# Self-attention on Trainium2: the last chunk of a pair's maxima taken one step earlier, and negated there

## The chip, the cores and the metric

The kernel runs on one core of a Trainium2 chip. The metric is the device time of one execution in microseconds, given as the median of several runs.

## The reference

A decoder layer in float32 for four sequences of 1024 tokens of width 256, in three parts, each followed by a residual sum and a layer norm: causal self-attention with 16 heads of 64 and rotary embedding, cross-attention that gathers at computed places, and a feed-forward part with fake quantisation. The change touches only the first:

```
q = (x @ wq.T + bq).reshape(Bx, Sx, H, DK).transpose(0, 2, 1, 3)     # k, v alike
q, k = _rope(q, k)
scores = jnp.einsum('bhqd,bhkd->bhqk', q, k)
scores = jnp.where(causal[None, None], -jnp.inf, scores)
attn = jax.nn.softmax(scores / math.sqrt(DK), axis=-1)
out = jnp.einsum('bhqk,bhkd->bhqd', attn, v)                         # then @ wo.T + bo
```

## The kernel before

Self-attention takes the first 1510 us or so of the program. Its work is cut into 16 groups (`GROUPS`: four sequences times four groups of four heads), and a group into two pairs of heads (`PAIRS` = 32 in all; pair `n` belongs to group `i = n // 2`, with `p = n % 2`). Both heads of a pair are worked on together.

The softmax is computed on transposed scores (keys on the partitions), so the maximum of each query has to be known before. It is found by a first, separate product of queries and keys: the nine `CHUNKS`, each a PSUM slot of 128 x 1024 values that holds one or two tiles of queries for both heads. TensorE writes a chunk (`max_chunk`, matmuls at L394), VectorE adds the causal mask where the chunk has corners (L633) and reduces it (L639, or L644 for parts of unequal width) in `maximum`. After the last chunk `negate` joins the halves (L650) and writes the negated maxima (`negmax`, L653).

In the pair itself, TensorE turns the negated maxima into a row in PSUM (`max_row`, L406), ScalarE copies the row (L507), and the row is added to every unit of scores by a second matmul (`shift`, L424) on top of the product of keys and queries (`scores`, L416). There are twelve such units (`NU`), two per step; s0 to s11 below. ScalarE takes the exponential of each (L518), GpSimd masks those on the diagonal (L761) and adds all up for the softmax's sums (L780), and TensorE weighs the values (`weigh`, L440).

A pair has six steps (`STEPS`, `m` = 0 to 5). The order of a step on TensorE is written out by hand: scores of units 2m and 2m+1; at step 0 the row of maxima and the last two weighings of the pair before; the two shifts; the weighings of the two units before; the chunks of the next pair's maxima that `CHUNKS_AT[m]` names; and one unit of other work (`FULL_AT`: projection of the next group's queries and keys at steps 0 to 3 of the first pair, output projection of the last group and values of the next at steps 0 to 3 of the second, L337 to L378). Steps 4 and 5 have no such unit.

All these outputs except those of `weigh` go through one ring of three PSUM slots of two banks (`SLOTS`), in the order that `slot_order` lists. `wait_slot` makes each use wait until the use three places before it has been read: scores by ScalarE's exponential, a chunk by VectorE's reduction (`s_mread`), the row by ScalarE's copy, a projection of queries and keys by VectorE's rotation. TensorE executes in program order, so whatever stands behind a waiting use waits with it.

VectorE's order is written by hand too: in each step the chunks of `CHUNKS_AT[m]`; at step 5 `negate`; then splits of the weights (`split`, L592 and L595: a float32 value as the sum of two parts), statistics or row normalisation of finished rows, the rotation or the values, at steps 4 and 5 of some pairs two pieces each of the split of x, and at step 4 `normalise` (L666), which multiplies the outputs of pair n-1 by the inverses of the sums. The split of x stands in pairs 5, 13 and 21, for the next sequence, and its last piece is needed by the projection of queries and keys in the next pair.

SyncE's queue stacks the rotated queries and keys into the operands (`stack`, L251). Before that it waits until all the scores of the pair that still uses them are done (`s_s`). After the split of x it loads the x of the sequence after (L243), which stands ahead of a stacking in the queue.

Of the kernel before, what the change touches and what calls it, by code (L numbers as in the profile page):

```python
# [27 lines left out]
PAIRS = 2 * GROUPS  # L28
# [4 lines left out]
NCH = len(CHUNKS)  # L33
PARTS = 2
STEPS = NU // 2
CHUNKS_AT = [range(0, 0), range(0, 2), range(2, 4), range(4, 6), range(6, 8), range(8, 9)]
QK_UNITS = 4
V_UNITS = 2
OUT_UNITS = 2
# [30 lines left out]
def slot_order():  # L70
# [3 lines left out]
    for n in range(PAIRS):  # L74
        i, p = divmod(n, 2)
        for m in range(STEPS):
# [3 lines left out]
            if n + 1 < PAIRS:  # L80
                order += [("max", n + 1, c) for c in CHUNKS_AT[m]]
            if FULL_AT[p][m]:
# [11 lines left out]
def attention(nc, dram, y, psum):  # L94

    ctx = ExitStack()
    with ctx:
# [217 lines left out]
        def _(pe):  # L315
# [67 lines left out]
            def max_chunk(n, c):  # L383

                p = n % 2
                if n == 0 and c == 0:
                    pe.wait_ge(s_top, 16 * STACK_DMAS)
                if c == (2 if n == 0 else 0):
                    pe.wait_ge(s_ops[p], 16 * STACK_DMAS * (n // 2 + 1))
                wait_slot(pe, "max", n, c)  # L390
                dst = slot("max", n, c)
                for qt, hf, col, width in chunk_parts(c):
                    for hh, rows in enumerate(HEADS):
                        last = nc.tensor.matmul(dst[:, hh, col:col + width], ops[p][rows, 0, qt * P:(qt + 1) * P],  # L394
                                                ops[p][rows, 1, hf * BANK:hf * BANK + width], start=True, stop=True)
                last.then_inc(s_m, 1)
# [67 lines left out]
            for n in range(PAIRS):  # L464
                i, p = divmod(n, 2)
                for m in range(STEPS):
# [13 lines left out]
                    if n + 1 < PAIRS:  # L480
                        for c in CHUNKS_AT[m]:
                            max_chunk(n + 1, c)
# [75 lines left out]
        def _(dve):  # L558
# [38 lines left out]
            def split_x(b, piece):  # L597
                hf, kt = divmod(piece, KT)
                if b and piece == 0:
                    dve.wait_ge(s_x, 16 * b)  # L600
                tok = HALVES[hf]
                split(xT[:, kt, tok], xT_hi[:, kt, tok], xT_lo[:, kt, tok], s_xs)

            def split_qk(i):
                dve.wait_ge(s_wqk, 32 * (i + 1))
                split(wqk[:, :, :], wqk_hi[:, :, :], wqk_lo[:, :, :], s_wqks)

            def split_v(i):
                dve.wait_ge(s_wv, 32 * (i + 1))
                split(wv[:, :, :], wv_hi[:, :, :], wv_lo[:, :, :], s_wvs)  # L610
# [11 lines left out]
            def maximum(n, c):  # L622

                dve.wait_ge(s_m, NCH * n + c + 1)
                src = slot("max", n, c)
                parts = chunk_parts(c)
                corners = causal_corners(c)
                if corners:
                    blocks = src.rearrange("p h (k q) -> p h k q", q=P)
                    step = corners[1] - corners[0] if len(corners) == 2 else 1  # L630
                    block = blocks[:, :, corners[0]:corners[-1] + 1:step, :]
                    mask = later[:, :].unsqueeze(1).unsqueeze(1).broadcast_to([P, 2, len(corners), P])
                    V.tensor_tensor(block, block, mask, ALU.add).then_inc(s_mmask, 1)  # L633
                    dve.wait_ge(s_mmask, len(MASKED) * n + MASKED.index(c) + 1)
                if parts[0][3] == parts[-1][3]:
                    place_of = [qt + TT // 2 * hf for qt, hf, col, width in parts]
                    step = place_of[-1] - place_of[0] if len(parts) == 2 else 1
                    width = parts[0][3]
                    V.reduce_max(maxes[:, :, place_of[0]:place_of[-1] + 1:step],  # L639
                                 src[:, :, 0:len(parts) * width].rearrange("p h (k q) -> p h k q", q=width),  # L640
                                 AX.X).then_inc(s_mread, PARTS)
                else:
                    for qt, hf, col, width in parts:
                        V.reduce_max(maxes[:, :, qt + TT // 2 * hf], src[:, :, col:col + width], AX.X)\  # L644
                         .then_inc(s_mread, PARTS // len(parts))

            def negate(n):

                dve.wait_ge(s_mread, PARTS * NCH * (n + 1))
                V.tensor_tensor(maxa[:, :, TT // 2:TT], maxa[:, :, TT // 2:TT], maxb[:, :, :], ALU.max).then_inc(s_mcomb, 1)  # L650
                dve.wait_ge(s_mcomb, n + 1)
                dve.wait_ge(s_row, n)
                V.tensor_scalar(negz[:, :, :, 0], maxa[:, :, :], -1.0, None, ALU.mult).then_inc(s_neg, 1)  # L653

            def invert(n):
                dve.wait_ge(s_dcol, 32 * (n + 1))
                dve.wait_ge(s_rrow, 16 * n)
                V.reciprocal(rcol[:, :, :], dcol[:, :, :]).then_inc(s_rcol, 1)
# [9 lines left out]
            def residual(i, u):  # L668

                b = i // NG  # L670
                dst = y[:, b * TT + u * (TT // 2):b * TT + (u + 1) * (TT // 2), :]
                if i % NG == 0:
                    dve.wait_ge(s_y, 16)
                    V.tensor_tensor(dst, dst, out_bias[:, :].unsqueeze(1).broadcast_to([P, TT // 2, E]), ALU.add)\
                     .then_inc(s_yb, 1)
                    dve.wait_ge(s_yb, OUT_UNITS * b + u + 1)
                dve.wait_ge(s_out, OUT_UNITS * i + u + 1)
                if i:
                    dve.wait_ge(s_res, OUT_UNITS * (i - 1) + u + 1)
                V.tensor_tensor(dst, dst, slot("out", i, u).rearrange("p h (t e) -> p (h t) e", e=E), ALU.add)\  # L680
                 .then_inc(s_res, 1)

            def row_statistics(b, half):

                dve.wait_ge(s_res, OUT_UNITS * NG * (b + 1))
                for t in range(4 * half, 4 * half + 4):
                    V.bn_stats(a_stats[:, t, :], y[:, b * TT + t, :]).then_inc(s_as, 1)
                if half:
                    dve.wait_ge(s_as, TT * (b + 1))
                    for t in range(TT):  # L690
                        ins = V.bn_aggr(a_mv[:, t, :], a_stats[:, t, :])
                    ins.then_inc(s_avar, 1)

            def normalise_rows(b, half):
                dve.wait_ge(s_astd, b + 1)
                for t in range(4 * half, 4 * half + 4):
                    ins = V.tensor_scalar(y[:, b * TT + t, :], y[:, b * TT + t, :], a_mv[:, t, 0:1], a_rstd[:, t:t + 1],
                                          ALU.subtract, ALU.mult)
                ins.then_inc(s_ax1, 1)
# [13 lines left out]
            for n in range(PAIRS):  # L713
                i, p = divmod(n, 2)
                for m in range(STEPS):
                    if n + 1 < PAIRS:
                        for c in CHUNKS_AT[m]:
                            maximum(n + 1, c)
                    if m == STEPS - 1 and n + 1 < PAIRS:
                        negate(n + 1)  # L720
                    if n == 0 and m == 0:
                        split_qk(1)
                    if p == 1 and m == 0:
                        if i + 1 < GROUPS:
                            split_v(i + 1)
                        if i >= NG and i % NG >= 2:
                            normalise_rows(i // NG - 1, i % NG - 2)
                    if p == 1 and m < 2 and i >= NG and i % NG == 1:
                        row_statistics(i // NG - 1, m)
                    if p == 1 and m == 1 and i + 2 < GROUPS:  # L730
                        split_qk(i + 2)
                    if FULL_AT[p][m]:
                        kind, u = FULL_AT[p][m]
                        if kind == "out" and i:
                            residual(i - 1, u)
                        if kind == "qk" and i + 1 < GROUPS:
                            rotate(i + 1, u)
                        if kind == "v" and i + 1 < GROUPS:
                            values(i + 1, u)
                    if p == 1 and m >= 4 and i % NG == 2 and i // NG + 1 < B:  # L740
                        for piece in range(2):
                            split_x(i // NG + 1, 2 * (m - 4) + piece)
                    if m == 2 and n:
                        invert(n - 1)
                    if m == 4 and n:
                        normalise(n - 1)
# [1548 lines left out]
```

## Time and profile before

| | |
|---|---|
| median of 3 runs | 2374.44 us (2371.68 to 2383.48) |
| the profiled execution | 2374.92 us |
| its span, first to last instruction | 2373.2 us |
| mean granted TensorE clock | 0.917 |
| TensorE busy | 1896.3 us (80%) |
| VectorE busy | 1580.8 us (67%) |
| GpSimd busy | 1175.9 us (50%) |
| ScalarE busy | 913.5 us (38%) |

An engine's busy time is a sum over the whole span; what an edit is worth has to be read from the stage in which it stands. In the timelines below a line gives the start in us, the duration in us (of a merged run of equal instructions, first start to last end), the engine, the line, the operation, and in brackets how long the engine was idle before it and which instruction released it. A TensorE clock of 1.00 is 2.4 GHz and of 0.50 is 1.2 GHz.

### The profile page before, as it was taken

The numbers are of one execution on the slowest core, as the hardware profiler recorded it, in microseconds if no ns is written. First come the engines' busy times: TensorE is split into PE (matmuls) and PEld (weight loads), VectorE is DVE, ScalarE is ACT, GpSimd is POOL, SyncE is SP. The second block draws the span as 40 slices with busy tenths as digits, with TensorE's granted clock in tenths as the row PEclk, the third lists the DMA queues.
The fourth block names the chain that finished last, engine by engine and source line by source line (L and its number), as shares of the span: only waits on it lengthen the run. The fifth ranks groups of instructions, "written<-read, shape, count | busy, mean of one in ns | idle before, by whom it ended". The sixth has DMA issues, their size and how long they took to land. (4 is left out here: it accounts for less than half of the span.)

```text
span 2373.2 us, 41594 instructions
## 1 busy us (share of the span) xinstructions
PE 1896.3 (80%) x16891; PEld 1130.9 (48%) x16891; DVE 1580.8 (67%) x2581; ACT 913.5 (38%) x1273; POOL 1175.9 (50%) x938
## 2 busy tenths in 40 slices
PE   6888878888878888888888898658787778884476
PEld 3444434444445444444444443446565566663332
DVE  6765656656656657666666663267868768778676
ACT  0222222222222222222222223156675765775376
POOL 0455436545644554555465456136555454646247
PEclk7999989999989999999999999779898898888686
DMA  7122112112221121121131121200000000100002
GB/s 216 28 57 52 41 52 70 41 39 56 54 56 41 43 65 41 43 65 37 39 72 39 39 47 34 59 5 7 2 2 7 2 2 2 41 2 2 2 1 71
DMA packets 57407, 93.39 MB, mean 39 GB/s; under 512 B 26624, under 2 KB 39040, under 8 KB 52864
## 3 DMA queue, kind: packets, MB, share of 16 engines
q1 hardware_dynamic: 48000, 90.47, 15.1%
q8 instruction: 134, 2.20, 0.4%
q10 hardware_dynamic: 9216, 0.27, 0.2%
q14 instruction: 57, 0.47, 0.1%
HBM read 52.43 MB, written 4.46 MB: 24 GB/s over the span
## 5 line engine op out<-in xcount | busy, mean ns | idle before, releaser
L780 POOL TENSOR_TENSOR acc<-acc,probs 128x1024 f32<-128x1024 f32 (+3 forms) x320 | 553.7, 1730 | 143.7 <-ACT probs L518 114.9
L518 ACT ACTIVATE probs<-psum 128x1024 f32<-128x1024 f32 (+3 forms) x384 | 290.5, 808 | 639.0 <-PE psum L424 639.0
L416 PE MATMUL psum<-operands 64*128 64x512 f32 (+3 forms) x1536 | 316.1, 517 | 59.8 <-DVE turned L587 23.5
L639 DVE TENSOR_REDUCE maxes<-psum 128x2 f32<-128x1024 f32 (+1 forms) x224 | 268.3, 1223 | 132.0 <-PE psum L394 121.8
L1322 ACT ACTIVATE onehot<-psum 128x1024 bf16<-128x1024 f32 x320 | 322.8, 1037 | 1.3 <-PE psum L1132 1.3
L1150 PE MATMUL psum<-pieces,onehot 128*128 128x64 bf16 x7680 | 296.1, 201 | 30.9 <-ACT vs L1329 24.1
L1150 PEld LDWEIGHTS psum<-pieces,onehot 128*128 128x128 bf16 x7680 | 267.6, 103 | 96.7 <-issue 46.5
L440 PE MATMUL psum<-probs,vals 128*64 128x512 f32 (+3 forms) x1536 | 293.8, 505 | 4.4 <-POOL probs L761 4.4
L1736 POOL TENSOR_TENSOR vs<-vs,wgt 128x1280 f32<-128x1280 f32 x64 | 156.9, 2452 | 261.4 <-DVE wgt L1579 261.4
L761 POOL TENSOR_SCALAR_AFFINE_SELECT probs<-probs 128x256 f32<-128x256 f32 x256 | 132.1, 528 | 278.2 <-ACT probs L518 278.2
L416 PEld LDWEIGHTS psum<-operands 64*128 64x128 f32 x1536 | 131.9, 187 | 202.2 <-issue 86.3
L777 POOL COPY acc<-probs 128x1024 f32<-128x1024 f32 x64 | 66.5, 1038 | 318.1 <-ACT probs L518 318.1
L1539 DVE TENSOR_TENSOR prod<-psum,xq 128x320 f32<-128x320 f32 x256 | 123.6, 488 | 114.3 <-PE psum L1150 109.5
L1132 PE MATMUL psum<-i0T,near 32*128 32x512 bf16 x640 | 133.5, 420 | 80.1 <-ACT onehot L1322 74.1
L633 DVE TENSOR_TENSOR psum<-psum,later 128x512 f32<-128x512 f32 (+1 forms) x160 | 93.8, 586 | 148.9 <-PE psum L394 148.9
L579 DVE SCALAR_TENSOR_TENSOR turned<-psum,bqk,rot 128x512 f32<-128x512 f32 x128 | 90.1, 745 | 146.4 <-PE psum L341 101.6
L1329 ACT ACTIVATE vs<-psum 128x320 f32<-128x320 f32 x256 | 114.8, 448 | 156.5 <-DVE prod L1539 156.2
L440 PEld LDWEIGHTS psum<-probs,vals 128*64 128x64 f32 x1536 | 95.6, 140 | 141.2 <-issue 131.6
L394 PE MATMUL psum<-operands 64*128 64x512 f32 (+3 forms) x768 | 118.0, 397 | 54.6 <-DVE turned L587 44.5
L378 PE MATMUL psum<-wo,ctxT 128*128 128x256 f32 x512 | 119.9, 388 | 26.9 <-ACT probs L518 15.7
L394 PEld LDWEIGHTS psum<-operands 64*128 64x128 f32 x768 | 59.9, 190 | 155.4 <-issue 89.5
L532 ACT ACTIVATE den_rows<-psum 128x1024 f32<-128x1024 f32 x32 | 32.8, 1024 | 250.5 <-PE psum L452 250.5
(220 smaller groups left out, 3181.4 us busy)
## 6 DMA issues: line engine op xcount, KB each, us to landing
operands<-turned SPq DMA_DIRECT2D x124, 256.0 KB, 4.3
rden<-inverse_rows SPq DMA_DIRECT2D x64, 256.0 KB, 3.8
wqk<-in_wqk SPq DMA_DIRECT2D x16, 512.0 KB, 3.2
wv<-in_wv SPq DMA_DIRECT2D x16, 256.0 KB, 2.6
y<-in_x SPq DMA_DIRECT2D x1, 4096.0 KB, 20.5
wo<-in_wo SPq DMA_DIRECT2D x16, 256.0 KB, 2.6
out<-res SPq DMA_DIRECT2D x16, 256.0 KB, 2.1
xT<-in_xT SPq DMA_DIRECT2D x3, 1024.0 KB, 6.7
```

What stands on the lines that cost most here:

```text
L394: last = nc.tensor.matmul(dst[:, hh, col:col + width], ops[p][rows, 0, qt * P:(qt + 1) * P], ops[p][rows, 1, hf * BANK:hf * BANK + width], ...
L416: nc.tensor.matmul(dst[:, hh, 0:width], ops[n % 2][rows, 1, kt * P:(kt + 1) * P].bitcast(F32), ops[n % 2][rows, 0, a:a + width].bitcast(F3 ...
L440: last = nc.tensor.matmul(obank[rows, hf, a - hf * BANK:BANK], vals[i % 2][:, kt, 2 * p + hh, :], probs[u % PBUF][:, hh, 0:width], start=k ...
L518: nc.scalar.activation(probs[u % PBUF][:, :, 0:width], slot("s", n, u)[:, :, 0:width], ACT.Exp, scale=1.0 / D ** 0.5).then_inc(s_exp, 1)
L639: V.reduce_max(maxes[:, :, place_of[0]:place_of[-1] + 1:step], src[:, :, 0:len(parts) * width].rearrange("p h (k q) -> p h k q", q=width), ...
L761: G.affine_select(block, block, [[0, 2], [1, P]], ALU.is_ge, 0.0, base=0, channel_multiplier=-1)\
L780: G.tensor_tensor(dst, dst, src, ALU.add).then_inc(s_acc, 1)
L1132: last = nc.tensor.matmul(bc[m % 2][:, hf * BANK:(hf + 1) * BANK], near[row:row + Q, NK * j + k, :], i0T[row:row + Q, hp // 2, :], start=T ...
L1150: last = nc.tensor.matmul(out, onehot[:, n % 2, k, tok:tok + P], pieces[b % 2][p][:, h, :, :].rearrange("p (s c) d -> p s (c d)", s=2), st ...
L1322: A.activation(onehot[:, n % 2, k, :], bc[m % 2], ACT.Relu).then_inc(s_oh, 1)
L1539: V.tensor_tensor(prod[u % 2][:, :, :].rearrange("p t (k d) -> p t k d", d=HD), slot("s", n, u)[:, :, 0:W].rearrange("p t (k d) -> p t k d ...
L1736: G.tensor_tensor(v, v, w.broadcast_to([P, TT * NK * 2, HD]), ALU.mult).then_inc(s_wm, 1)
```

## The change

The ninth chunk (number 8) of the next pair's maxima moves from step 5 to step 4, in the ring's order, on TensorE and on VectorE, since all three loops read `CHUNKS_AT`. The negation moves on VectorE from step 5 to step 4, right behind that chunk. TensorE's row stays where it is, in step 0 of the next pair.

```
-CHUNKS_AT = [range(0, 0), range(0, 2), range(2, 4), range(4, 6), range(6, 8), range(8, 9)]
+CHUNKS_AT = [range(0, 0), range(0, 2), range(2, 4), range(4, 6), range(6, 9), range(9, 9)]
...
                     if n + 1 < PAIRS:
                         for c in CHUNKS_AT[m]:
                             maximum(n + 1, c)
-                    if m == STEPS - 1 and n + 1 < PAIRS:
+                    if m == STEPS - 2 and n + 1 < PAIRS:
                         negate(n + 1)
```

The uses of the ring around the end of a pair, before and after:

```
before: s8 s9 max6 max7 | s10 s11 max8 | s0 s1 row ...
after:  s8 s9 max6 max7 max8 | s10 s11 | s0 s1 row ...
```

## Rows read from the trace of the kernel before

**Rows 1.** The page, busy time of each engine (share of the span) xinstructions.

```profile
PE 1896.3 (80%) x16891; PEld 1130.9 (48%) x16891; DVE 1580.8 (67%) x2581; ACT 913.5 (38%) x1273; POOL 1175.9 (50%) x938
```

**Rows 2.** Waits, 0 to 1560 us: who waited for whom, us in total, times, longest.

```profile
PE psum L406 <- DVE negmax L653: 58.0, 32, 5.6
```

**Rows 3.** Timeline of PE, 774 to 812 us, row of pair 16.

```profile
790.70 0.64 PE L406 MATMUL psum<-ident,negmax 128*64 128x128 bf16 x16 [1.68 <-DVE negmax L653]
```

**Rows 4.** Timeline of DVE, 774 to 812 us, ahead of pair 16.

```profile
785.36 1.29 DVE L644 TENSOR_REDUCE maxes<-psum 128x2 f32<-128x256 f32 x2
786.57 1.96 DVE L666 TENSOR_TENSOR ctxT<-osum,rden 128x1024 f32<-128x1024 f32 x1
```

**Rows 5.** Timeline of all engines, 733 to 755 us, into pair 15.

```profile
740.71 1.23 DVE L639 TENSOR_REDUCE maxes<-psum 128x2 f32<-128x1024 f32 x1 [0.67 <-PE psum L394]
...
741.99 0.49 PE L416 MATMUL psum<-operands 64*128 64x128 f32 x4 [0.67 <-DVE maxes L639]
...
742.57 1.29 DVE L644 TENSOR_REDUCE maxes<-psum 128x2 f32<-128x256 f32 x2
...
743.78 1.57 DVE L666 TENSOR_TENSOR ctxT<-osum,rden 128x1024 f32<-128x1024 f32 x1
...
744.23 0.50 PE L394 MATMUL psum<-operands 64*128 64x512 f32 x2
...
744.57 1.67 PE L416 MATMUL psum<-operands 64*128 64x512 f32 x8
...
745.27 0.42 DVE L633 TENSOR_TENSOR psum<-psum,later 128x256 f32<-128x256 f32 x1
...
747.26 0.20 DVE L653 TENSOR_SCALAR negmax<-maxes 128x16 bf16<-128x16 f32 x1
...
747.52 0.64 PE L406 MATMUL psum<-ident,negmax 128*64 128x128 bf16 x16 [1.29 <-DVE negmax L653]
```

**Rows 6.** Timelines of DVE and of PE, 88 to 101 us, into pair 1.

```profile
92.68 1.29 DVE L644 TENSOR_REDUCE maxes<-psum 128x2 f32<-128x256 f32 x2
...
97.50 0.64 PE L406 MATMUL psum<-ident,negmax 128*64 128x128 bf16 x16 [1.16 <-DVE negmax L653]
```

**Rows 7.** Timelines of DVE, SyncE and PE, 676 to 722 us, into pair 14.

```profile
693.87 0.69 DVE L595 TENSOR_TENSOR xT_low<-xT,xT_high 128x512 fp32r<-128x512 f32 x1
...
706.21 1.41 DVE L579 SCALAR_TENSOR_TENSOR turned<-psum,bqk,rot 128x512 f32<-128x512 f32 x2 [11.64 <-DMA operands<-turned]
...
695.27 4.60 SPq L251 DMA_DIRECT2D operands<-turned  x4
...
710.53 1.33 PE L394 MATMUL psum<-operands 64*128 64x128 f32 x6 [6.73 <-DVE turned L587]
```

**Rows 8.** Timelines of DVE and of PE, 1053 to 1085 us, into pair 22.

```profile
1056.07 1.29 DVE L644 TENSOR_REDUCE maxes<-psum 128x2 f32<-128x256 f32 x2
...
1066.63 0.69 DVE L595 TENSOR_TENSOR xT_low<-xT,xT_high 128x512 fp32r<-128x512 f32 x1
...
1065.29 1.06 PE L406 MATMUL psum<-ident,negmax 128*64 128x128 bf16 x16 [5.56 <-DVE negmax L653]
...
1069.38 0.47 PE L337 MATMUL psum<-xT_high,wqk_high 128*128 128x512 f32 x1 [0.89 <-ACT probs L518]
```

**Rows 9.** Two lines: duration ns min/median/max, first and last start.

```profile
L666 DVE TENSOR_TENSOR ctxT<-osum,rden x32: 1226/1612/2042, 130.1 to 1507.8; 128x1024 f32<-128x1024 f32 x32
...
L595 DVE TENSOR_TENSOR xT_low<-xT,xT_high x16: 691/692/1631, 31.5 to 1066.6; 128x512 fp32r<-128x512 f32 x16
```

**Rows 10.** Timeline of DVE, 774 to 812 us, the rotation in pair 16.

```profile
797.10 1.41 DVE L579 SCALAR_TENSOR_TENSOR turned<-psum,bqk,rot 128x512 f32<-128x512 f32 x2 [6.46 <-PE psum L341]
```

**Rows 11.** The page, DMA issues: count, KB each, median us to landing.

```profile
operands<-turned SPq DMA_DIRECT2D x124, 256.0 KB, 4.3
```

**Rows 12.** Two periods from row to row: busy us by engine, granted clock, DMA.

```profile
790.70:837.07 46.37, 39.11 (x218) 20.38 (x218) 32.19 (x45) 12.10 (x16) 23.20 (x21) 0.96 0.19 44
880.26:925.46 45.20, 37.52 (x217) 19.23 (x217) 32.09 (x45) 12.10 (x16) 23.18 (x21) 1.00 0.19 45
```

More of the change, by code:

```diff
@@ L35 @@
 STEPS = NU // 2
-CHUNKS_AT = [range(0, 0), range(0, 2), range(2, 4), range(4, 6), range(6, 8), range(8, 9)]
+CHUNKS_AT = [range(0, 0), range(0, 2), range(2, 4), range(4, 6), range(6, 9), range(9, 9)]
 QK_UNITS = 4
@@ L718, in _ @@
                             maximum(n + 1, c)
-                    if m == STEPS - 1 and n + 1 < PAIRS:
+                    if m == STEPS - 2 and n + 1 < PAIRS:
                         negate(n + 1)
```

## The prediction

> **What bounds the kernel now.** I read the page's busy times first: TensorE (PE) is busy 80% of the span, VectorE (DVE) 67% [rows 1]. A change that adds and removes no instruction can only move PE's waits. The list of waits, cut to the attention stage (0 to 1560 us), names the one near the change: the matmuls of the row of maxima (L406) stood 58.0 us in 32 places behind `negmax` (L653), 5.6 us at most [rows 2]. The timeline gives the single waits before these 32 groups: one of 0.47 (pair 0, outside the loop), one of 1.16 (pair 1), fifteen of 1.29 to 1.33 (pairs 3, 5, ..., 29 and pair 8), twelve of 1.67 to 1.75 (the other even pairs and pair 31) and three of 5.56 us (pairs 6, 14, 22); they sum to 58. Rows 3 and 4 show one of the twelve, rows 5 one of the fifteen, rows 8 one of the three.
>
> Why PE waits there: VectorE reduces chunk 6, masks and reduces chunk 7 (L633, L644), normalises the context (L666), masks and reduces chunk 8 and negates, without a gap of over 0.1 us, and PE starts 0.05 us after the last [rows 3 to 5]. The row is set by VectorE's queue.
>
> **The change part by part.** Nothing is added or removed. Two things move: on VectorE chunk 8 (0.42 + 1.23 us) and the negation go ahead of `normalise(n-1)` and, in three pairs, of splits of x; on PE the matmuls of chunk 8 go ahead of the scores of units 10 and 11 (s10, s11). The second also moves the uses of the PSUM ring of three slots, where a use waits for the reader of the use three places before. Before: s10 waits for the exponential of s9, s11 for the reduction of chunk 6, chunk 8 for chunk 7. After: chunk 8 waits for s9, s10 for chunk 6, s11 for chunk 7. That is a new wait: s11 is one place further on in VectorE's queue, and behind it in PE's order stand both shifts, the weighing of units 8 and 9, the next pair's s0 and s1, and then the row.
>
> A. The negation. VectorE can go on straight after chunk 7. From the mask of chunk 8 to the end of the negation it takes 745.27 to 747.46 = 2.19 us, so `negmax` is ready at 743.78 + 2.19 = 745.97 instead of 747.46 [rows 5].
>
> B. s11. Before, chunk 6's reduction ends at 740.71 + 1.23 = 741.94 and s11 starts at 741.99: 0.05 us from a reduction to PE. After, s11 starts at 742.57 + 1.29 + 0.05 = 743.91. From the start of s11 to the end of s1 PE needed 741.99 to 744.57 + 1.67 = 746.24, 4.25 us; of this chunk 8's matmuls (744.23 to 744.57, 0.34) now stand earlier: 3.91 us. The row then starts at 743.91 + 3.91 = 747.82, against 747.52: **+0.30 us** [rows 5]. The negation is 1.85 us ahead of it and no longer matters. Chunk 8's 0.34 us lie in the wait for chunk 6 (0.67 us before s11 [rows 5]) and cost nothing; uncovered they cost 0.34. s0 needs chunk 8 read, at 743.78 + 0.53 + 1.23 = 745.5, and starts at 747.82 - 1.67 = 746.15: covered by 0.6 us.
>
> C. The same for the twelve: 785.36 + 1.29 + 0.05 + 3.91 = 790.61 against 790.70: **-0.09 us** [rows 3, 4]. The two kinds differ in what the normalisation had cost, 1.57 or 1.96 us. Pair 1 has none: 92.68 + 1.29 + 0.05 + 3.91 = 97.93 against 97.50, +0.43 us [rows 6].
>
> Sum of the regular boundaries: 14 x 0.30 + 0.25 (pair 8, normalisation 1.61) + 0.43 - 12 x 0.09 = **+3.8 us**. What follows a row (ACT's copy, shifts, exponentials, projection) hangs on it, and the next rotation on VectorE waits for PE (6.46 us idle [rows 10]), so a delay of the row goes through in full. Ends: a reduction may reach PE 0.15 us earlier or later, 28 x 0.15 = 4 us to either side.
>
> D. Pairs 6 and 14. Here two splits stood ahead of the normalisation too. The row starts some 4 us earlier (by the like pair 22: 1056.07 + 1.29 + 0.05 + 3.91 = 1061.32 against 1065.29 [rows 8]). But nothing that ends last hangs on it: the next group's projection needs the last split, at the end of the same gapless VectorE queue (693.87 + 0.69 = 694.56 in either order); SyncE then issues xT and, from 695.27, the operands (4.60 us), the rotation waits for these until 706.21, and PE's maxima for the rotation until 710.53, idle for 6.73 us [rows 7]. The 4 us become a longer wait there. Worth 0, apart from E.
>
> E. Contention on VectorE in the same three places. The normalisation takes 1.23 to 2.04 us over the stage, 1.74 there; a split's subtraction 0.69 in the median and 1.63 at most [rows 9], the latter there, while GpSimd masks and adds. With 2.1 us of PSUM work moved to the front, the normalisation should stand behind the end of GpSimd's adds: 1.74 - 1.23 = 0.5 us for each of three. Ends: 0, and 0.5 + 2 x (1.63 - 0.69) = 2.4 us if the subtractions came free too; I take 0.5, since the adds move back as well, with the exponentials of units 10 and 11.
>
> The Trainium skill ("SBUF — State Buffer", section "Who interferes with whom") says that a VectorE instruction with two SBUF inputs contends with a GpSimd instruction that reads SBUF, while a reduction never does. By that rule no term of B or C could grow from GpSimd's moved adds, as both rest on reductions and on PE, and E may be anything between its ends. The trace agrees: 1.23 to 2.04 us for one form of normalisation [rows 9], 1.23 and 1.29 us for the reductions wherever they stand [rows 4 to 6].
>
> F. Pair 22 has the splits but no load of xT behind them. The next group's projection began at 1069.38 and needs the last split, done at 1066.63 + 0.69 = 1067.32 [rows 8]. The earlier row lets it start at 1067.4: -2.0, with E -2.5 us. Ends: 0 (if a low clock eats it) and -4.5.
>
> G. The SyncE queue. It holds the stacking of operands until all scores of a pair are done; s11 comes 743.91 - 741.99 = 1.9 us later, so do these four DMAs. Issued from 785.46 for 3.12 us, they land 4.3 us after each issue [rows 11], by 792.9, and 794.8 after; the rotation that needs them starts at 797.10, held by PE [rows 10]. Two us of cover: 0. Without it up to 1.9 us for each of 15 groups.
>
> **Sum**: +3.8 - 1.0 (E, pairs 6 and 14) - 2.5 = +0.3 us on the profiled execution's 2374.92 us (span 2373.2 and 1.7 around it). The median of the three runs is 2374.44, 0.5 lower; I predict **2375 us**, no change that a measurement of this kernel can tell (0.5%, 12 us).
>
> **Rivals.**
> 1. The wait is simply removed: 58.0 - 0.5 us go, 2317 us, if s10 and s11 don't bind. For it: the largest wait of PE for VectorE in this stage [rows 2]. Against: VectorE has no gap between chunk 6 and chunk 7, so s11 cannot start before 743.9. 6%.
> 2. Slower by TensorE's clock. PE's idle time now lies in one wait of 1.5 to 1.9 us at s11 soon after that of s10. The granted clock fell to 0.50 (1.2 GHz) in stretches after waits of this stage; a period with one such stretch (mean clock 0.96) took 46.37 us, one without (1.00) 45.20: 1.17 us each [rows 12]. If each of the 28 boundaries brought one more, 33 us: 2408. It decides from 10 boundaries on. For: the waits before s11 now come close together. Against: the idle time per boundary is the same sum, and 1.29 and 1.68 us in one piece mostly left the clock at 1.00. 7%.
> 3. The delayed stacking (G) comes to bind: 15 x 1.9 = 28 us at most, 2403. It decides only if landing takes 2.3 us more than now. 2%.
> 4. The change doesn't bring what it says, since PE asks for the negated maxima no earlier. That is my forecast in the regular pairs. A partial form, faster by the whole 4 us of pairs 6, 14 and 22, gives 2374.9 + 3.8 - 12 = 2367, still within 0.5%.
>
> **How the numbers follow.** Forecast (within 0.5%, with rival 4): 82%; rival 1: 6%; rival 2: 7%; rival 3: 2%; a gain I don't see: 3%. Faster 0.09, same 0.82, slower 0.09. Range: regular boundaries 4 us either way, the three split boundaries -8 to +3, low-clock stretches, which may come or go, some 6 us; and the runs of before themselves lie from 2371.68 to 2383.48. So 2366 to 2384.
>
> **What would show it.** The idle time before L406 behind `negmax` falls from 58 to under 2 us; that before L416 behind a maximum (L639, L644) grows to some 55 us; the row starts 3.9 us after s11; at pairs 6 and 14 PE's maxima still wait for a rotation that waited for the operands. I am wrong if s11 starts less than 1.5 us after s10, if the granted clock of the stage differs by over 0.02, or if the rotation begins to wait for DMA in ordinary groups.

## The result: slower, by TensorE's clock

The changed kernel takes 2414.96 us (median of 4 runs, 2411.64 to 2420.36) against 2378.96 us for the kernel before beside it: a ratio of 1.0179, 95% interval 1.0149 to 1.0208 (the two medians alone give 1.0151). I had predicted 2375 us in a range of 2366 to 2384, and given 7% to the rival that turned out to be the case. The profiled execution took 2411.64 us. Of the runs below, one of the kernel before (2946.74 us) and one of filled_wait (9743.97 us) stand far from all others and enter no ratio.

The page of the changed kernel, first its busy times, then the costliest groups (busy us, mean ns | idle before, us). The instruction counts are those of [rows 1]:

```profile
PE 1942.5 (81%) x16891; PEld 1141.2 (47%) x16891; DVE 1581.1 (66%) x2581; ACT 913.4 (38%) x1273; POOL 1175.9 (49%) x938
...
L416 PE MATMUL psum<-operands 64*128 64x512 f32 (+3 forms) x1536 | 333.0, 540 | 102.0 <-DVE maxes L644 38.0
...
L440 PE MATMUL psum<-probs,vals 128*64 128x512 f32 (+3 forms) x1536 | 325.8, 550 | 4.4 <-POOL probs L761 4.4
```

TensorE does the same instructions and is busy for 46 us longer. Its weight loads (PEld) take 10 us more; no other engine's busy time moved by over 1 us. The scores (L416) had been busy 316.1 us before and the weighings (L440) 293.8: +17 and +32 us.

Its waits in the stage of self-attention (0 to 1560 us; us in total, times, longest):

```profile
PE psum L416 <- DVE maxes L644: 38.0, 31, 1.2
PE psum L416 <- DVE maxes L639: 29.6, 36, 1.2
...
PE psum L406 <- DVE negmax L653: 0.5, 1, 0.5
```

The wait behind `negmax`, 58.0 us in [rows 2], is gone but for 0.5 us, and a wait of s11 for chunk 7 (L644) stands in its place, 1.23 us at every boundary. That half went as forecast in place, less so in size: the waits behind a maximum come to 67.6 us, and I had said some 55, and the one at s11 was to be 1.5 to 1.9 us. The stage seen as a whole, from the first row of maxima to the last, is in these two lines, of the kernel before and then of the changed one (length, busy us of PE, PEld, DVE, ACT, POOL, then the granted clock, DMA share, GB/s):

```profile
49.57:1458.22 1408.65, 1193.61 (x7080) 642.79 (x7081) 897.41 (x1197) 373.74 (x494) 727.84 (x626) 0.97 0.21 50
```

```profile
50.04:1504.05 1454.01, 1247.40 (x7080) 656.07 (x7080) 901.92 (x1199) 373.58 (x494) 728.77 (x626) 0.94 0.20 48
```

The stage is 45.4 us longer, PE is busy 53.8 us longer in it, so PE's idle time even fell by 8.4 us, and the mean granted clock went from 0.97 to 0.94, more than the 0.02 that I had named as a sign of being wrong. The clock of all runs says the same: averaged over the whole program it was 0.898 to 0.901 in the four runs of the changed kernel, and 0.910 to 0.929 in the 53 of the kernel before that stood beside the experiments. (The rest of the program was 9 us shorter in this execution; between executions of all the kernels here it lies between 905 and 915 us and carries nothing of the change.)

One boundary of the changed kernel, into pair 18, on the timeline of PE. It answers to [rows 3, 5]:

```profile
894.16 1.01 PE L394 MATMUL psum<-operands 64*128 64x512 f32 x8
896.05 0.70 PE L416 MATMUL psum<-operands 64*128 64x256 f32 x4 [0.88 <-DVE maxes L639]
897.98 0.73 PE L416 MATMUL psum<-operands 64*128 64x128 f32 x4 [1.23 <-DVE maxes L644]
898.49 0.54 PE L424 MATMUL psum<-bias,first_rows 64*128 64x256 bf16 x4
898.96 2.96 PE L440 MATMUL psum<-probs,vals 128*64 128x512 f32 x8
901.85 1.77 PE L416 MATMUL psum<-operands 64*128 64x512 f32 x8
903.56 0.64 PE L406 MATMUL psum<-ident,negmax 128*64 128x128 bf16 x16
```

And on VectorE's:

```profile
896.63 1.29 DVE L644 TENSOR_REDUCE maxes<-psum 128x2 f32<-128x256 f32 x2
```

s11 starts at 897.98, 0.06 us after the end of chunk 7's reduction, as step B has it. But from s11 to the row it is 5.58 us and not 3.91: s11 takes 0.73 instead of 0.49 us, the shifts 0.54 instead of 0.33, the weighings of units 8 and 9 take 2.96 instead of 1.72. The clock says why; the stretch of the two waits, then the one from s11 on, then the one with the row:

```profile
895.10:898.00 2.90, 0.80 (x8) 0.33 (x6) 2.87 (x5) 0.00 (x0) 2.76 (x2) 1.00 0.00 0
898.10:901.50 3.40, 3.40 (x16) 1.27 (x16) 2.94 (x5) 0.87 (x2) 2.48 (x4) 0.50 0.39 82
902.00:905.50 3.50, 3.03 (x34) 1.55 (x36) 0.00 (x0) 1.02 (x1) 1.44 (x2) 1.00 0.93 187
```

TensorE is busy for 0.80 of 2.9 us, and then works at 1.2 GHz (0.50) just when it has work. Counted over the stage from the clock's record, there are 41 stretches of low clock (177 us) instead of 15 (79 us). 26 of the 41 begin between 0.6 us before and 0.9 us after the start of s11, where the kernel before has none; the other 15 match its 15. The changed kernel has its own control in this: at the five boundaries without a fall (pairs 1, 4, 12, 27 and 30) the row starts 3.94 us after s11, at 20 of those with one 5.4 to 5.6 us, and at the six where the low clock lasts twice as long 6.9 to 7.0 us. The waits of s10 and s11 are the same at all of them to 0.01 us (but for pair 8, with 1.23 us at s10), so they do not tell at which boundary the clock falls; what does is not known.

### The profile page after: what moved, and what is told of

It is laid out like the page before. It is cut to its first block and busy times, and to the rows that moved or that the text cites. A ratio compares the mean times of both kernels' runs of the same rounds, so it can differ in the third digit from the quotient of the medians.

```text
span 2409.9 us, 41594 instructions
## 1 busy us (share of the span) xinstructions
PE 1942.5 (81%) x16891; PEld 1141.2 (47%) x16891; DVE 1581.1 (66%) x2581; ACT 913.4 (38%) x1273; POOL 1175.9 (49%) x938
## 5 line engine op out<-in xcount | busy, mean ns | idle before, releaser
L780 POOL TENSOR_TENSOR acc<-acc,probs 128x1024 f32<-128x1024 f32 (+3 forms) x320 | 568.0, 1775 | 143.5 <-ACT probs L518 114.7
L416 PE MATMUL psum<-operands 64*128 64x512 f32 (+3 forms) x1536 | 333.0, 540 | 102.0 <-DVE maxes L644 38.0
L440 PE MATMUL psum<-probs,vals 128*64 128x512 f32 (+3 forms) x1536 | 325.8, 550 | 4.4 <-POOL probs L761 4.4
L761 POOL TENSOR_SCALAR_AFFINE_SELECT probs<-probs 128x256 f32<-128x256 f32 x256 | 116.6, 468 | 316.2 <-ACT probs L518 316.2
L416 PEld LDWEIGHTS psum<-operands 64*128 64x128 f32 x1536 | 133.9, 196 | 287.1 <-issue 115.0
L440 PEld LDWEIGHTS psum<-probs,vals 128*64 128x64 f32 x1536 | 101.1, 148 | 159.2 <-issue 132.2
L394 PE MATMUL psum<-operands 64*128 64x512 f32 (+3 forms) x768 | 110.0, 389 | 57.9 <-DVE turned L587 47.8
L337 PE MATMUL psum<-xT_high,wqk_high 128*128 128x512 f32 x240 | 107.9, 450 | 20.4 <-ACT probs L518 19.1
```

The source lines that it names most:

```text
L416: nc.tensor.matmul(dst[:, hh, 0:width], ops[n % 2][rows, 1, kt * P:(kt + 1) * P].bitcast(F32), ops[n % 2][rows, 0, a:a + width].bitcast(F3 ...
L440: last = nc.tensor.matmul(obank[rows, hf, a - hf * BANK:BANK], vals[i % 2][:, kt, 2 * p + hh, :], probs[u % PBUF][:, hh, 0:width], start=k ...
L761: G.affine_select(block, block, [[0, 2], [1, P]], ALU.is_ge, 0.0, base=0, channel_multiplier=-1)\
L780: G.tensor_tensor(dst, dst, src, ALU.add).then_inc(s_acc, 1)
```

## The experiments

The theory: the waits moved as predicted, at no cost of their own; the loss is the low clock that follows two waits close together. The rivals: VectorE's new order (contention with GpSimd), or the moved wait itself. The table has what each run gave; the ratio is to the kernel before on the same chip, the stretches of low clock are those that begin between the first and the last row of maxima, in the one profiled execution of each.

| kernel | median us | ratio (95%) | low stretches, at s11 | stage us |
|---|---|---|---|---|
| before | | 1 | 15, 0 | 1408.7 |
| after | 2414.96 | 1.0179 (1.0149 to 1.0208) | 41, 26 | 1454.0 |
| chunk_only | 2410.48 | 1.0197 (1.0161 to 1.0233) | 36, 26 | 1447.7 |
| vector_order_only | 2367.26 | 0.9990 (0.9969 to 1.0010) | 16, 0 | 1403.4 |
| filled_wait | 2371.14 | 1.0002 (0.9975 to 1.0028) | 13, 0 | 1412.2 |
| filled_once | 2391.71 | 1.0080 (1.0050 to 1.0109) | 23, 9 | 1420.9 |
| before_filled | 2368.84 | 0.9980 (0.9962 to 0.9998) | 15, 0 | 1406.3 |
| weigh_in_wait | 2366.61 | 0.9987 (0.9965 to 1.0008) | 16, 0 | 1400.4 |
| row_between | 2364.28 | 0.9960 (0.9944 to 0.9976) | 17, 0 | 1396.5 |
| row_between_spread | 2363.35 | 0.9948 (0.9928 to 0.9969) | 19, 0 | 1398.3 |

The kernel before had a median of 2371.68 us beside chunk_only, vector_order_only, filled_wait and weigh_in_wait, of 2375.36 us beside the other four, and of 2378.96 us beside the changed one. The ratios are not the quotients of these medians, and lie up to 0.0033 from them.

### chunk_only: the negation back in step 5

```
-                    if m == STEPS - 2 and n + 1 < PAIRS:
+                    if m == STEPS - 1 and n + 1 < PAIRS:
                         negate(n + 1)
```

> The changed kernel with the negation (and nothing else) put back into step 5, behind the normalisation. Clock theory: the loss comes from the two waits that the moved chunk puts close together ahead of s10 and s11, after which TensorE runs at 1.2 GHz for a stretch at most boundaries; the negation is not on the path (it would be ready at 743.78 + 1.66 + 2.19 = 747.6 us against a row at 747.8). So about the changed kernel's 2415 us (2405 to 2420), about 40 stretches of low clock. Rival, that the negation's and the normalisation's new order on VectorE costs the time (contention with GpSimd): back to about 2379 us.

As slow as the change, with as many stretches at s11 (26, not all at the same boundaries). The half of the change that moves the negation is no cause of the loss; the chunk alone makes it. It is not quite off the path, as I had said: with the negation back in step 5 the row waits for it at eight boundaries, 6.6 us in all.

### vector_order_only: only VectorE's order

```
+VECTOR_CHUNKS_AT = [range(0, 0), range(0, 2), range(2, 4), range(4, 6), range(6, 9), range(9, 9)]
...
-                        for c in CHUNKS_AT[m]:
+                        for c in VECTOR_CHUNKS_AT[m]:            # in VectorE's loop alone
...
-                    if m == STEPS - 1 and n + 1 < PAIRS:
+                    if m == STEPS - 2 and n + 1 < PAIRS:
                         negate(n + 1)
```

> The kernel before, with only VectorE's order changed: it takes chunk 8 and the negation ahead of the splits of x and the normalisation; the ring and TensorE's order stay. Clock theory: no new wait ahead of s10 and s11, so the low-clock stretches stay at about 17, and the row comes when chunk 8's matmuls are read: 744.7 + 2.2 = 746.9 instead of 747.5 in fifteen boundaries, 789.7 instead of 790.7 in twelve, less 0.4 us each if the small L650 meets GpSimd as in pair 1: 10 to 21 us faster than before, 2358 to 2369 us. Rival (VectorE's order is what slows): about 2415 us.

Not slower, so the rival falls; but the gain of 10 to 21 us was expected too large: the interval of 0.9969 to 1.0010 leaves 7 us at most. The row's waits behind `negmax` fall from 58.0 to 38.7 us, but some 12.6 us of that lie at the three boundaries with splits (5.56 to 1.35 us each), where step D had it worth nothing at two. Two timelines of this kernel show why so little is left of the others, PE's and VectorE's, into pair 16:

```profile
785.20 0.64 PE L407 MATMUL psum<-ident,negmax 128*64 128x128 bf16 x16 [1.36 <-DVE negmax L654]
```

```profile
782.39 0.43 DVE L634 TENSOR_TENSOR psum<-psum,later 128x256 f32<-128x256 f32 x1 [0.91 <-PE psum L395]
782.92 1.23 DVE L640 TENSOR_REDUCE maxes<-psum 128x2 f32<-128x1024 f32 x1
784.18 0.17 DVE L651 TENSOR_TENSOR maxes<-maxes 128x8 f32<-128x8 f32 x1
784.38 0.77 DVE L654 TENSOR_SCALAR negmax<-maxes 128x16 bf16<-128x16 f32 x1
```

With the normalisation out of the way, VectorE waits 0.91 us for chunk 8's matmuls, and the negation (0.20 us in [rows 5]) takes 0.77 us. The row's wait goes from 1.68 us [rows 3] only to 1.36. The negation is that long at 12 boundaries; at the others it takes 0.20 us as before, and there the wait of the kind of [rows 5] still only goes from 1.29 to 1.17 us.

### filled_wait: the same order, with TensorE kept busy

```
+                if u == NU - 2:
+                    for _ in range(FILL):                         # FILL = 3
+                        for hh, rows in enumerate(HEADS):
+                            nc.tensor.matmul(dst[:, hh, width:2 * width], ops[n % 2][rows, 1, kt * P:(kt + 1) * P].bitcast(F32),
+                                             ops[n % 2][rows, 0, a:a + width].bitcast(F32), start=True, stop=True)
                 for hh, rows in enumerate(HEADS):
                     nc.tensor.matmul(dst[:, hh, 0:width], ops...      # s10 itself
```

> The changed kernel with extra matmuls on TensorE ahead of s10 (three more copies of s10's own score matmuls into the unused half of its PSUM slot, some 1.1 us per pair; their results are read by nobody). They lie in the wait for chunk 7, so the path s11 to row stays. Clock theory: TensorE is busy where it idled, the low-clock stretches fall from 41 towards 17 and the time to 2375 to 2390 us, in spite of more work. Rival (the loss is in waits or in the order, not in the clock): 2415 us or more.

This is the decisive run: TensorE does 372 matmul instructions more in the stage (12 a pair) and the kernel is 1.7% faster than the changed one, back at the time of before and a little below the 2375 us at which my range began, with no low stretch at s11. Its PE timeline into pair 18, and the two stretches that answer to the first two of the changed kernel above:

```profile
875.10 1.57 PE L419 MATMUL psum<-operands 64*128 64x256 f32 x12 [0.88 <-DVE maxes L645]
876.50 1.02 PE L422 MATMUL psum<-operands 64*128 64x256 f32 x8
877.36 0.33 PE L430 MATMUL psum<-bias,first_rows 64*128 64x256 bf16 x4
877.62 1.72 PE L446 MATMUL psum<-probs,vals 128*64 128x512 f32 x8
879.27 1.77 PE L422 MATMUL psum<-operands 64*128 64x512 f32 x8
880.98 0.64 PE L407 MATMUL psum<-ident,negmax 128*64 128x128 bf16 x16
```

```profile
874.20:877.10 2.90, 2.02 (x20) 1.53 (x18) 2.87 (x5) 0.00 (x0) 2.76 (x2) 1.00 0.00 0
877.20:880.60 3.40, 3.40 (x24) 1.42 (x24) 2.90 (x5) 0.87 (x2) 2.83 (x4) 1.00 0.56 116
```

The weighings are back at 1.72 us. And with the clock out of it, the arithmetic of steps B to D can be seen bare: the periods from row to row are 43.1 and 45.5 us in the undisturbed pairs, against 43.2 and 45.2 before. The forecast of those was -0.09 and +0.30 us.

### filled_once and before_filled: a third of the filler, and the control

filled_once is filled_wait with `FILL = 1`; before_filled is the kernel before with the same block and `FILL = 3`.

> The changed kernel with one extra copy of s10's score matmuls ahead of s10 instead of three (some 0.37 us of the 2.1 us of waits at s10 and s11; results read by nobody). Clock theory: the fall of the clock hangs on how much idle time lies together; with a third of the filler TensorE idles for 1.75 us of that stretch, about what the timeline of the kernel before has around its row, so most of the low-clock stretches should go: 2375 to 2395 us. Rival, that any filler works only in proportion to the idle time that it takes: 2415 - 43/3 = 2400 us.

> Control: the kernel before with the same three extra copies ahead of s10. There s11 waited only 0.67 us and the row waits for VectorE, so 0.4 us of delay of s11 is covered. Clock theory: the filler brings nothing where the clock did not fall: 2366 to 2380 us, 12 to 17 low-clock stretches in the stage. Rival (filler is good in itself): as much faster than before as the filled changed kernel was than the changed one, 40 us, 2330 us.

In between, by both the time and the stretches: nine of them at s11. Two stretches of filled_once at the same place as above, into pair 18, one of the nine:

```profile
883.20:886.10 2.90, 1.23 (x12) 0.71 (x10) 2.87 (x5) 0.00 (x0) 2.76 (x2) 1.00 0.00 0
886.20:889.60 3.40, 3.40 (x16) 1.10 (x16) 3.06 (x5) 0.87 (x2) 2.70 (x4) 0.53 0.55 113
```

So with PE busy 0.80, 1.23 and 2.02 of the 2.9 us ahead of s11, the clock fell at 26, 9 and 0 of 31 boundaries. It is a matter of degree: the ratio 1.0080 is 19 us over before, where the rival that counts idle time alone wanted about 29. I had expected most of the stretches to go, which is so (17 of 26), though the time comes out near the upper end of my figure. The control lies 0.2% below before (0.9962 to 0.9998), nowhere near the 40 us that filler gives the changed kernel: filler does not help by itself.

### weigh_in_wait: useful work in the wait

```
+                    if m == STEPS - 1:
+                        weigh(n, 2 * m - 2)
                     scores(n, 2 * m)
+                    if m == STEPS - 1:
+                        weigh(n, 2 * m - 1)
                     scores(n, 2 * m + 1)
...
-                    if m:
+                    if 0 < m < STEPS - 1:
                         weigh(n, 2 * m - 2)
```

> The changed kernel with useful work in the wait: at step 5 the weighing of unit 8 goes ahead of s10 and that of unit 9 ahead of s11, instead of both behind the shifts. s11 still starts at 743.9 (chunk 7), but the row follows it by 3.91 - 1.66 = 2.25 us, at 746.16, just behind the negation at 745.97. Clock theory: row 1.7 us earlier than in the changed kernel at 28 boundaries and the low clock gone: 2375 - 46 = 2330 us (2320 to 2345). Rival (no clock effect): 2415 - 46 = 2369 us.

Half right. The low stretches at s11 are gone and the change's loss with them, but 2330 us was wrong by 37 us: I had moved s11's followers forward without asking what their own slots wait for. Its PE timeline into pair 16:

```profile
783.02 0.49 PE L416 MATMUL psum<-operands 64*128 64x128 f32 x4 [0.37 <-DVE maxes L648]
783.34 0.33 PE L424 MATMUL psum<-bias,first_rows 64*128 64x256 bf16 x4
784.68 1.77 PE L416 MATMUL psum<-operands 64*128 64x512 f32 x8 [1.01 <-DVE maxes L643]
786.39 0.64 PE L406 MATMUL psum<-ident,negmax 128*64 128x128 bf16 x16
```

s0 takes the slot of chunk 8 and waits 1.01 us for its reduction; in step B that was covered by 0.6 us, and 1.66 us of cover had been taken away. In the new order the row cannot come sooner than the end of chunk 8's reduction and s0 and s1 (1.7 us).

### row_between and row_between_spread: a version that beats both

The row between s0 and s1, in the ring and on TensorE, on top of weigh_in_wait; row_between_spread also takes chunk 6 in step 3 in the second pair of each group.

```
                     scores(n, 2 * m)
                     if m == STEPS - 1:
                         weigh(n, 2 * m - 1)
+                    if m == 0:
+                        max_row(n)
                     scores(n, 2 * m + 1)
...                                                              # row_between_spread, indexed by p, m
+CHUNKS_AT = [[range(0, 0), range(0, 2), range(2, 4), range(4, 6), range(6, 9), range(9, 9)],
+             [range(0, 0), range(0, 2), range(2, 4), range(4, 7), range(7, 9), range(9, 9)]]
```

> The changed kernel with the weighings of units 8 and 9 in the waits of step 5, and the row of maxima between s0 and s1 instead of behind both (in the ring too). In the run with the weighings alone s0 waited 1.0 us for chunk 8, and the row stood behind s1 0.9 us further on although the negation was ready 0.42 us after chunk 8. Now the row starts 0.8 us earlier, and s1 and the weighings of 10 and 11 cover ACT's copy (0.47 us idle before). Expected 0.5 us per boundary, 31 x 0.5 = 16 us off 2366: 2350 us (2343 to 2360). Rival, that the clock falls again in the wait of s0: 2366 us or more.

> As row_between, and in the second pair of each group chunk 6 is taken in step 3 instead of 4, where VectorE idled 3.3 us. Then only chunks 7 and 8 lie between step 4's start and s0, the queue of VectorE ends 1.2 us earlier at 16 boundaries, and the waits of s11 and s0 go: up to 1.0 us each for 12 to 15 of them, 2335 to 2345 us. Rival, that step 3 gets a wait of its own (the values' slot behind chunk 6): 2350 us as without it.

row_between is faster than before by 0.4% (0.9944 to 0.9976), though at 2364 us outside my 2343 to 2360. The step from weigh_in_wait brings less than was hoped, 0.2 us a pair and not 0.5: the periods of undisturbed pairs are 42.4 and 44.8 us, against 42.6 and 45.0. In its timeline the 0.47 us behind ACT's copy are gone:

```profile
873.43 1.13 PE L417 MATMUL psum<-operands 64*128 64x512 f32 x4 [1.01 <-DVE maxes L645]
874.49 0.64 PE L407 MATMUL psum<-ident,negmax 128*64 128x128 bf16 x16
875.05 0.92 PE L417 MATMUL psum<-operands 64*128 64x384 f32 x4
875.90 0.87 PE L441 MATMUL psum<-probs,vals 128*64 128x256 f32 x8
876.70 0.55 PE L425 MATMUL psum<-bias,first_rows 64*128 64x512 bf16 x4
```

The spread adds nothing that these runs can tell (0.9948, 0.9928 to 0.9969; stage 1398.3 us), where I had expected 2335 to 2345 us. In its waits the rival shows: 13.9 us in 15 places of a wait that row_between has not, of the values' matmuls behind a maximum, against 13.0 us that the scores' waits behind maxima lost (45.4 to 32.4):

```profile
PE psum L364 <- DVE maxes L646: 13.9, 15, 0.9
```

## Why the prediction was wrong, step by step

- **A, B and C** (the negation's wait goes, s11's wait comes, +0.30 and -0.09 us per boundary) were right, in the changed kernel for the places of the waits, in filled_wait for the periods too. The 0.05 us from a reduction to PE (0.06) and the 3.91 us from s11 to the row (3.94) held in the changed kernel where the clock was 1.00.
- **The step that failed is the clock, which the sum puts at nothing**: it has no term for it, the range allows "some 6 us" for stretches that "may come or go", and rival 2 got 7% because "the idle time per boundary is the same sum, and 1.29 and 1.68 us in one piece mostly left the clock at 1.00". In its place the runs showed 26 new stretches of low clock, some 42 us. Neither the sum nor the longest single piece foretold them: both fell, the sum by 8.4 us over the stage and the longest piece at an ordinary boundary from 1.68 to 1.23 us. In the kernel before, the idle time around the row of pair 16 lies in three waits with work between, and the clock stays; the second line is the sparsest 2.9 us there:

```profile
789.00:794.10 5.10, 1.90 (x31) 1.08 (x29) 1.58 (x3) 2.24 (x3) 2.23 (x4) 1.00 0.51 103
788.90:791.80 2.90, 1.22 (x26) 0.90 (x24) 1.60 (x3) 0.42 (x1) 2.21 (x3) 1.00 0.90 181
```

PE is busy for 1.22 us of those 2.9, and in the changed kernel for 0.80, since two of its waits have only s10 between them. I had called the short distance a point for the rival, and then let the sum outweigh it. But the busy time alone does not settle it. Over 5.1 us up to s11 the changed kernel is busy for longer than the one before around its row:

```profile
892.90:898.00 5.10, 3.00 (x22) 1.08 (x18) 3.20 (x5) 1.06 (x2) 4.23 (x4) 1.00 0.18 60
```

And filled_once, with 1.23 us in its 2.9, had a fall at nine of 31 boundaries, where the kernel before with 1.22 us had one at its twelve of this kind (pair 10, 1.6 us after the row). The sparse stretch of before holds the row's bf16 matmuls and that of the changed kernel fp32 scores; whether the kind of work counts was not tested. What the runs show is that the place of the loss is the stretch from s10 to s11, and that work put there takes it away.

The price I gave a stretch, 1.17 us, was also too low: (1454.0 - 1412.2) / 26 = 1.6 us, because it falls where PE sets the pace with the work behind a wait, fp32 matmuls at half rate (weighings 2.96 for 1.72 us). The number of boundaries that rival 2 needed was 10; it was 26. The Trainium skill ("TensorE: Matmul & The Clock Gate", section "HAM oscillation — how this bites in real kernels") tells of waits of 3 to 5 us for DMA between bursts of matmuls that lower the clock each time round a loop. The trace agrees that it comes back round after round, at 26 of 31 boundaries, and differs in the wait: none of those at s10 and s11 was over 1.23 us.
- **D** was right: in filled_wait, the period up to pair 6's row falls from 47.1 to 43.1 us (4.0, as worked out), and the next grows from 54.7 to 58.2. The 4 us went into a wait of PE for the last split (3.11 us, where it had waited 0.89 us for ScalarE) and into a longer wait for the rotation (8.1 to 8.7 us at pair 6, 6.7 to 9.9 at pair 14).
- **E** was right for the normalisation (1.22 us instead of 1.74 in filled_wait, at pair 22), but a subtraction of a split still took 1.64 us there. Its net effect is in D: 101.8 us for the two periods together before, 101.3 in filled_wait.
- **F** came out at its upper end, 0, and not at -2.0. The projection in filled_wait did start at the last split, but then ran at the low clock; PE's timeline and two stretches:

```profile
1068.13 0.76 PE L338 MATMUL psum<-xT_high,wqk_high 128*128 128x512 f32 x1 [3.11 <-DVE xT_low L601]
```

```profile
1064.00:1068.00 4.00, 0.56 (x6) 0.12 (x4) 3.93 (x6) 2.64 (x4) 2.00 (x3) 0.81 0.37 74
1068.00:1072.00 4.00, 3.87 (x9) 3.12 (x10) 0.03 (x1) 0.00 (x0) 2.76 (x2) 0.50 0.02 6
```

The two periods there are 43.1 + 51.6 = 94.7 us, against 47.1 + 47.5 = 94.6 before.
- **G** was right: the rotation waits for DMA in three places as before (32.6 us in the changed kernel, 32.3 before).

## What to carry to other kernels

A wait that is moved is not worth the same at its new place, even when its length and the sum of all waits stay: look at how much work TensorE has between neighbouring waits, since a sparse stretch ahead of a burst can make the burst itself slow, though how sparse is too sparse these runs do not tell. When two waits come close together, put work between them, useful work from behind them if its inputs are ready; here even useless matmuls paid for the whole loss. And when followers of a wait are moved up, ask of each of them again what it waits for: the next bound of the ring stood 1 us behind the one that was removed.

## What the runs showed of the hardware

- At s11 of the changed kernel the clock fell with no wait of over 1.23 us ahead of it, after 2.9 us with PE busy for 0.80 us. With 1.23 us of work in this place (filled_once) it fell at 9 boundaries instead of 26, with 2.02 us (filled_wait) at none; around the row of the kernel before, with 1.22 us in 2.9, at one of twelve.
- In the changed kernel it fell at the same point of the order, within 1 us of the start of s11, at 26 of 31 boundaries, and PE was at full clock again by the row, 5.4 to 7.0 us after s11.
- Three more copies of s10's 64x256 float32 score matmuls per pair of heads cost the kernel before no time that could be measured (0.9980, 0.9962 to 0.9998): they lie where TensorE waits.
- A VectorE operation of 128x16 elements (`negmax`) took 0.20 us in all 32 places of the kernel before, 0.74 to 0.77 us in 12 of vector_order_only, and 1.24 to 1.25 us in 13 of chunk_only; that GpSimd's work beside it is the cause was not tested.
